# Attention outputs normalised in the attention stage on GpSimd, layer norm inside the turn plan, weight loads issued by ScalarE, output loads reordered

## The reference

```
s   = attention(xn)                    # 32 query heads, 8 key/value heads, head size 32, rotary, causal
g   = silu(ffn(xn))
out = x + s * g
```

```
t = layer_norm(xn)[:, -1, :] @ agg_w + agg_b
repeat 4 times: t = t + gelu(layer_norm(t) @ d1_w + d1_b) @ d2_w + d2_b
broadcast = t @ bc_w + bc_b
ffn = layer_norm(xn + sigmoid(xn @ gate_w + gate_b) * broadcast)
```

## Time and profile before

| | us |
|---|---|
| median of three runs | 2880.41 |
| profiled execution | 2904.24 |
| its span | 2902.5 |
| busy TensorE | 2643.2 (91%) |
| busy VectorE | 1714.5 (59%) |
| busy GpSimd | 1297.7 (45%) |
| busy ScalarE | 1055.4 (36%) |
| TensorE's mean granted clock | 0.954 |

### The profile page before, as it was taken

One profiled execution on the slowest core, in us unless ns is written; L12 is line 12 of the kernel. 1 busy time (PEld: TensorE's weight loads), 2 busy tenths in 40 slices (PEclk: granted clock), 3 DMA queues, 4 the chain that ended last, 5 costly groups with the idle time before them and its releaser, 6 DMA issues. The chain is left out here.

```text
span 2902.5 us, 46017 instructions
## 1 busy us (share of the span) xinstructions
PE 2643.2 (91%) x14400; PEld 1712.5 (59%) x14400; DVE 1714.5 (59%) x3448; ACT 1055.4 (36%) x1715; POOL 1297.7 (45%) x562
## 2 busy tenths in 40 slices
PE   5999999969999999999999999995688788898887
PEld 4888888844444444444444444442577676676775
DVE  6455444356555655566556655653666667676666
ACT  2111111106666565665666556662211111111111
POOL 0211211127788678877888688872111111111111
PEclk9999999979999999999999999997799999899998
DMA  6444444365654565556455545564678677567766
GB/s 232 167 175 172 166 173 174 138 201 182 189 154 152 166 189 153 153 167 186 152 156 167 184 152 157 167 189 137 138 123 116 111 123 123 111 124 124 123 114 121
DMA packets 235894, 450.04 MB, mean 155 GB/s; under 512 B 17528, under 2 KB 101720, under 8 KB 235860
## 3 DMA queue, kind: packets, MB, share of 16 engines
q1 hardware_dynamic: 162468, 397.68, 43.3%
q0 software_dynamic: 73392, 51.91, 14.4%
HBM read 334.42 MB, written 114.58 MB: 155 GB/s over the span
## 5 line engine op out<-in xcount | busy, mean ns | idle before, releaser
L867 DVE CUSTOM_DVE_ANT_0 bcast<-mxp,mask_q 128x128 f32<-128x128 f32 (+7 forms) x1054 | 751.9, 754 | 506.4 <-PE mxp L976 283.5
L796 ACT ACTIVATE pr<-stp 128x512 f32<-128x512 f32 x1152 | 670.3, 596 | 529.1 <-PE stp L985 351.6
L985 PE MATMUL stp<-qs,ks 97*128 97x512 f32 x1152 | 522.5, 461 | 19.2 <-ACT pr L796 14.8
L1385 PE MATMUL gp<-g,xa 128*128 128x512 f32 x1536 | 395.3, 421 | 128.9 <-DMA xa<-xt_scratch 117.5
L426 PE MATMUL eo<-xt,w 128*128 128x512 f32 x1920 | 449.2, 393 | 3.6 <-DVE xt L369 3.6
L749 POOL TENSOR_TENSOR acc<-acc,pr 128x2048 f32<-128x2048 f32 x96 | 439.7, 4580 | 24.7 <-ACT pr L796 14.5
L985 PEld LDWEIGHTS stp<-qs,ks 97*128 97x128 f32 x1152 | 214.7, 189 | 384.1 <-ACT pr L796 275.8
L1385 PEld LDWEIGHTS gp<-g,xa 128*128 128x128 f32 x1536 | 313.5, 206 | 210.1 <-issue 108.0
L426 PEld LDWEIGHTS eo<-xt,w 128*128 128x128 f32 x1920 | 359.1, 189 | 77.5 <-issue 4.0
L1385 PE MATMUL op<-o,ya 128*128 128x512 f32 x1536 | 356.2, 391 | 21.6 <-DVE ya L1326 21.6
L1385 PEld LDWEIGHTS op<-o,ya 128*128 128x128 f32 x1536 | 290.3, 189 | 82.6 <-DVE ya L1326 22.0
(11 more groups left out here) (139 smaller groups left out, 2788.0 us busy)
## 6 DMA issues: line engine op xcount, KB each, us to landing
wch<-in_d_w SPq DMA_DIRECT2D x132, 1024.0 KB, 8.0
qs<-q_scratch SPq DMA_DIRECT2D x201, 256.0 KB, 7.3
xa<-xt_scratch POOLq DMA_DIRECT2D x66, 512.0 KB, 9.0
xt_scratch<-xt SPq DMA_DIRECT2D x16, 2048.0 KB, 14.6
q_scratch<-r SPq DMA_DIRECT2D x64, 512.0 KB, 3.2
o_rinv<-r_scratch SPq DMA_DIRECT2D x33, 512.0 KB
yr<-y_scratch POOLq DMA_DIRECT2D x33, 512.0 KB, 6.5
xs<-in_x SPq DMA_DIRECT2D x33, 512.0 KB, 10.7
```

Of the source, the lines that this page charges most:

```text
L796: nc.scalar.activation(pr[half][:, :, at:at + P], stp[u % 2][:].rearrange("p (h t) -> p h t", h=REP), ACT.Exp, scale=SCALE).then_inc(act_d ...
L867: last = nc.vector.tensor_tensor_reduce(out=bcast[:, k % 2, hh * step:hh * step + w], in0=mxp[k % 2][:, hh * step:hh * step + w], in1=mask ...
L985: last = nc.tensor.matmul(bank, ks[par][:, j * P:(j + 1) * P], qs[par][:, :, i * P:(i + 1) * P], start=True, stop=i != j)
L1385: last = nc.tensor.matmul(bank[:, cols], lhs[pa][:, k, :], ws[pw][:, k, cols], start=(k == 0 and (pa, pw) == (0, 0)), stop=(k == KT - 1 an ...
```

## The change

The sums of a half are stored to a small `s_scratch` as soon as they are there, and loaded back as 128 partitions of 16 numbers (`spread_sums`); VectorE inverts these (`rc 1` in slot 27, `rc 0` in slot 33), SyncE stores the inverses and loads them repeated over each head's partitions (`spread_inverse`), and GpSimd multiplies `ys` with them (`normalise`) before y is stored: half 1 between its third and fourth large addition, half 0 after the fourth. SyncE's order of a turn changes with it: y of half 0 is now stored in the turn after, both spreads stand at the turn's end, ahead of the next turn's load of `ks`. The output stage drops its sums, inversion, spread load and multiplication.

The weights of the recurrent part are issued by ScalarE, behind its copy of the first burst and, for the second, behind the exponential of unit 12. In the last two turns of a step the layer norm is in the plan (`ls`, `l0`, `lc`, `l1`, `lv`, `lt`; only in the odd turn), for which the last iteration of the loop over chunks is unrolled (`turns`). In the output stage GpSimd waits for `y2_done` and issues `load_ya` ahead of `load_xa`.

```diff
@@ -81,21 +81,23 @@
 12: mx 5, pv 0 3, cy 0
 13: mx 6
 14: ss 1
-15: mx 7
+15: mx 7, ls
 16: mx 8
-18: mx 9
+18: mx 9, l0, lc
 19: mx 10, ge
 20: ss 0, mx 11
 21: pv 1 0, pv 1 1
 22: mx 12
 23: mx 13
-24: pv 1 2
+24: pv 1 2, l1, lv
 25: mt 0, mx 14
 26: mx 15
+27: rc 1
 28: pv 1 3, mx 16
 29: mx 17
 31: mx 18, pv 1 4
-33: mx 19
+32: lt
+33: mx 19, rc 0
 34: pv 1 5
...
+SPREAD = REP * HALF // P
...
+        sr = [sb(f"sr{i}", [P, SPREAD], F32) for i in range(2)]
+        rr = [sb(f"rr{i}", [P, SPREAD], F32) for i in range(2)]
+        rinv = [sb(f"rinv{i}", [P, HALF], F32) for i in range(2)]
...
-        use = {"fa": 0, ("mt", 1): 1, "fb": 2, "ft": 3, ("ss", 1): 4, ("ss", 0): 5, ("mt", 0): 6}
+        uses = [{"fa": 0, ("mt", 1): 1, "fb": 2, "ft": 3, ("ss", 1): 4, ("ss", 0): 5, ("mt", 0): 6},
+                {"fa": 0, ("mt", 1): 1, "fb": 2, "ft": 3, ("ss", 1): 4, "l0": 5, ("ss", 0): 6, "l1": 7, ("mt", 0): 8}]
+
+        def turns(engine, turn):
+            with engine.Fori(0, STEPS) as s:
+                with engine.Fori(0, CH - 1) as c:
+                    for par in range(2):
+                        turn(s, c, par, uses[0])
+                for par in range(2):
+                    turn(s, CH - 1, par, uses[par])
 
         def products(e, n):
...
-            def store_sums(half, slot):
-                sp.dma_start(s_d[:, bass.ds(slot, 1), half * HALF:(half + 1) * HALF].rearrange("h a t -> h (a t)"),
-                             sm[half][0:P:HD, :]).then_inc(s_out[half], 16)
+            def spread_sums(half, k, tu):
+                sp.wait_ge(tr_free, tu + 2)
+                sp.dma_start(s_d[half], sm[half][0:P:HD, :]).then_inc(s_out[half], 16)
+                sp.wait_ge(s_out[half], 16 * k + 17)
+                sp.dma_start(sr[half][:], s_d[half].rearrange("h (a u) -> (h a) u", u=SPREAD)).then_inc(sr_in[half], 16)
+
+            def spread_inverse(half, k):
+                sp.wait_ge(rc_done, 2 * k + 2 - half)
+                sp.dma_start(r_d[half].rearrange("h (a u) -> (h a) u", u=SPREAD), rr[half][:]).then_inc(r_out[half], 16)
+                sp.wait_ge(r_out[half], 16 * k + 17)
+                rows = r_d[half].unsqueeze(1)
+                sp.dma_start(rinv[half][:], rows.to_broadcast([REP, HD, HALF])).then_inc(rb_in[half], 16)
...
+                sp.wait_ge(st_done, NST * n + 2)
+                load_k(nxt, (n + 1) % GROUPS)
+                load_q(1, nxt, it if par == 0 else (it + 1) % (GROUPS // 2))
+                sp.wait_ge(pv_done, products((1, 7), n))
+                load_v(nxt, (n + 1) % GROUPS)
+                sp.wait_ge(tr_free, tb + use[("mt", 1)] + 2)
+                move_mt(1, par)
+                cn = (c + par) % CH
+                sp.wait_ge(yn_done, 2 * n + 1)
+                store_y(0, n)
+                sp.wait_ge(st_done, NST * n + HALF_ST + 1)
+                load_q(0, par, (it + 1) % (GROUPS // 2))
+                if par == 1:
+                    sp.wait_ge(hp_done, it + 1)
+                    sp.dma_start(b1c[:], d1_b[bass.ds(cn, 1)].rearrange("a p k -> (a p) k")).then_inc(b1_in, 16)
+                spread_sums(1, n, tb + use[("ss", 1)])
+                spread_sums(0, n, tb + use[("ss", 0)])
+                sp.wait_ge(tr_free, tb + use[("mt", 0)] + 2)
+                move_mt(0, nxt)
+                spread_inverse(1, n)
+                sp.wait_ge(yn_done, 2 * n + 2)
+                store_y(1, n)
+                spread_inverse(0, n)
+
+            turns(sp, turn)
             sp.wait_ge(tr_full, LAST)
             sp.dma_start(picks, pick).then_inc(c_in, 16)
...
+            spread_sums(1, GROUPS, LAST + 2)
+            spread_inverse(1, GROUPS)
+            sp.wait_ge(yn_done, 2 * GROUPS + 1)
+            store_y(0, GROUPS)
...
+            def normalise(half, n):
+                pool.wait_ge(ys_done, 2 * n + 3 - half)
+                pool.wait_ge(rb_in[half], 16 * (n + 1))
+                nc.gpsimd.tensor_tensor(ys[half][:], ys[half][:], rinv[half][:], ALU.mult).then_inc(yn_done, 1)
...
+                    nc.gpsimd.tensor_tensor(acc[:], other, pr[1][:, :, at:at + HALF], ALU.add).then_inc(add_done, 1)
+                    if j == 3:
+                        if "l1" in use:
+                            ln_pool(s + 1, tb + use["l1"])
+                        normalise(1, n)
...
+            def load_w(burst, c, cw, par):
+
+                for kh in range(2):
+                    r = kh * 512 + burst * 256
+                    src = d2_w[bass.ds(c * D + r, 256), :] if par == 0 else d1_w[r:r + 256, bass.ds(cw * D, D)]
+                    nc.scalar.dma_start(wch[burst][:, 2 * kh:2 * kh + 2, :],
+                                        src.rearrange("(k p) n -> p k n", p=P)).then_inc(w_in[burst], 16)
...
+                        if e[0] == "fc":
+                            copy_burst(tb + use["fa"])
+                            load_w(0, c, cw, par)
+                        elif e[0] == "ft":
+                            act.wait_ge(tr_full, tb + use["fb"] + 1)
+                            load_w(1, c, cw, par)
...
-            def layernorm_scale(tu, k, base):
-                dve.wait_ge(tr_full, tu + 2)
-                nc.vector.tensor_scalar(ve[:], trp[:, 0:B], EPS_F, None, ALU.add).then_inc(ln_ve, 1)
+            def layernorm_var(tu):
+                dve.wait_ge(tr_full, tu + 1)
+                nc.vector.tensor_scalar(ve[:], trp[:, 0:B], EPS_F, None, ALU.add).then_inc(tr_free, 1)
+
+            def layernorm_scale(k, base):
                 dve.wait_ge(ln_rs, k + 1)
-                nc.vector.tensor_tensor(cen[:], cen[:], rows(rs[:]), ALU.mult).then_inc(tr_free, 1)
-                dve.wait_ge(tr_free, tu + 3)
+                link(nc.vector.tensor_tensor(cen[:], cen[:], rows(rs[:]), ALU.mult), base)
                 link(nc.vector.tensor_tensor(cen[:], cen[:], bc(fvec[:, 1, :], B), ALU.mult), base)
                 nc.vector.tensor_tensor(t_in[:, :, 0:B], cen[:], bc(fvec[:, 2, :], B), ALU.add).then_inc(t_done, 1)
+
+            def reciprocals(half, k):
+                dve.wait_ge(sr_in[half], 16 * (k + 1))
+                dve.wait_ge(r_out[half], 16 * k + 1)
+                nc.vector.reciprocal(rr[half][:], sr[half][:]).then_inc(rc_done, 1)
 
...
+                        elif e[0] == "ls" and "l0" in use:
+                            link(nc.vector.tensor_tensor(th[:], th[:], bc(fvec[:, 3, :], B), ALU.add), base)
+                            layernorm_sum()
+                        elif e[0] == "lc" and "l0" in use:
+                            layernorm_centre(tb + use["l0"], base)
+                        elif e[0] == "lv" and "l1" in use:
+                            layernorm_var(tb + use["l1"])
+                        elif e[0] == "lt" and "l1" in use:
...
+                        elif e[0] in ("l0", "l1") and e[0] in use:
+                            k = int(e[0] == "l1")
+                            mean(tb + use[e[0]], s2 if k else s1, (s + 1) * 2 + k + 1)
...
-                for k, v in enumerate((s1, s2)):
-                    mean(TR0 + s * TR_STEP + NT * TRN + k, v, (s + 1) * 2 + k + 1)
...
             for n, (src, _, w2, k) in enumerate(pieces):
-                if n == 2:
-                    spread(0, 0)
-                    load_sums(1)
...
-                    spread(1 - par, n + 1)
-                    load_sums((n + 2) % TILES)
...
             with pool.Fori(0, TILES) as n:
+                pool.wait_ge(y2_done, n + 1)
+                load_ya((n + 1) % TILES)
                 pool.wait_ge(g_done, n + 1)
                 load_xa((n + 1) % TILES)
                 power(n, 0)
                 power(n, 1)
-                pool.wait_ge(y2_done, n + 1)
-                load_ya((n + 1) % TILES)
...
-            act.wait_ge(yn_done, 1)
+            act.wait_ge(ya_in, 16)
...
-                    act.wait_ge(yn_done, n + 2)
+                    act.wait_ge(ya_in, 16 * (n + 2))
...
-            normalise(0)
...
-                    invert(n + 1)
...
-                    normalise(n + 1)
```

More of the change, by code:

```diff
@@ L539, in attention_phase @@
         s_out = [sem(f"a_s_out{i}") for i in range(2)]
+        sr_in = [sem(f"a_sr_in{i}") for i in range(2)]
+        r_out = [sem(f"a_r_out{i}") for i in range(2)]
+        rb_in = [sem(f"a_rb_in{i}") for i in range(2)]
+        rc_done, yn_done = sem("a_rc"), sem("a_yn")
         b1_in, c_in = sem("a_b1_in"), sem("a_c_in")
@@ new lines, in turn @@
+            def turn(s, c, par, use):
+                it = s * CH + c
+                n = it * 2 + par
+                nxt = 1 - par
+                tb = trb(s, c, par)
+                sp.wait_ge(st_done, NST * n + 2)
[21 more added lines that the diff above has]
+                spread_inverse(0, n)
@@ L681, in _ @@
             for half in range(2):
-                sp.wait_ge(y_out[half], 16 * (GROUPS + half) + 1)
+                sp.wait_ge(y_out[half], 16 * (GROUPS + 1) + 1)
                 sp.wait_ge(s_out[half], 16 * (GROUPS + half) + 1)
@@ L751, in _ @@
```

(15 more changed lines are left out.)

379 lines of the change are left out of this document (149 added, 230 removed).

## The result

The changed kernel takes 2962.8 us (median of 4 runs, 2958.3 to 2969.6), the one before 2882.6 in the same measurement: ratio 1.029, 95% interval 1.026 to 1.031. It is slower; I had forecast 2842 and faster.

A forecast was written before the change was run, and what follows sets the result against it. TensorE was taken as the attention's bound, with some 55 of 400 us idle in the output stage. Terms -16 + 25 + 3 + 2 - 12 - 35 - 5 = -38 took 2880.4 to 2842 us; range 2770 to 2930, own range 2800 to 2872.

The forecast's parts named there:

- The chain of inverse sums on SyncE's queue: Attention turns: stores, waits and spread loads delay `ks`; TensorE waits 0.8 us per group, +25 us, bounds 0 and +93.
- rival A: Attention turns: spread loads land in 5 to 6 us, TensorE waits 3 us per group; 2912 us in all, chance 0.15.
- Weights' loads from ScalarE: Attention turns: issue time on ScalarE, 0 to 63 us if unhidden, nearly all hidden by its waits for TensorE: +3 us.
- Layer norm: Attention step ends: three gaps of 8.62 us between turns go, 3.3 us per step comes back: -16 us, between 0 and -23.
- Tiles: Output stage: spread load, reciprocal and multiplication go, `xa` still waits some 5 us every second tile: -35 us, bounds -105 and +16.
- Rival D: Output stage: all loads hide, 23.3 to 24.5 us per tile and no slow clock; 2762 us in all, chance 0.10.
- Rival B: Attention turns: VectorE's reciprocal waits for GpSimd's additions, 3.2 us per group; 2945 us in all, chance 0.15.
- Rival C: Output stage: loads in the new order collide as before, tiles +16 instead of -35; 2893 us in all, chance 0.10.
- Handover: Attention to output stage: spread hold, first multiplication and handshake go, `xa` of tile 1 comes later: -12 us, bounds -5 and -17.
- End of the attention: Stage end: bias product's input no longer waits behind a layer norm, but a last chain is added: +2 us, bounds -6 and +8.
- a wait for `acc`: Attention turns: two added GpSimd multiplications per group delay the late additions whose sum TensorE wants at slot 14: cost 0.
- End: Kernel's end: the last `yr` multiplication and its wait for a load, before the last store, go: -5 us.

The follow-up runs named there:

- the chain repaired: Changed kernel with both reciprocals in slot 27 and both stores, then both spread loads, behind the transposed maxima: 2809.0 us, ratio 0.974.
- the best kernel: Changed kernel with both inverses together in slot 27 and ScalarE's weight loads moved to slots 12 and 18: 2768.9 us, ratio 0.960.
- two stores: Kernel before, with SyncE held each turn by two 16 KB stores and their waits ahead of the `ks` load: 2966.5 us, ratio 1.030.
- four: Kernel before, with SyncE held each turn by four 16 KB stores and their waits ahead of the `ks` load: 3098.8 us, ratio 1.074.

## Why the prediction was wrong

**The step that failed: "The chain of inverse sums on SyncE's queue".** It had the right mechanism and place, and rival A said what comes of it. The term was +25 us, bounds 0 and +93; it measured 200 (2962.8 - 2763.3). Three durations in it were too short. From the first spread load to y's store, behind which the second chain stands, it took 6.3 to 6.7 us, where I had 5.0: the load took 4.8 to 5.2 to its use, and I took the 3.6 of a `ks` load for it. The second store and wait took 1.8 us, not 1.40, since y's store is ahead of it in the queue; I had taken, where nothing is ahead. So `ks` was issued 3.0 us later, not 1.3. And it landed in 4.4 to 6.3 us, not 3.6: I wrote that 256 KB now lie ahead of it and gave them no time. The wait is 5.0 us in the turn shown and 4.9 on average of the 28 turns that have one, not 0.8. A plain turn is 7.7 us longer (48.06 against 40.37), so 2.8 go beside the wait, with a clock of 0.93 for 0.99; a part of them may be the early weights', which this kernel doesn't separate. I priced a microsecond of wait at one, although the output stage showed what a wait does to the product behind it: held by stores alone, it cost 1.7 to 1.8. Rival A, with spread loads of 5 to 6 us, took 3 us per turn, for the same omissions. It named what happened; I gave it 0.15. (Its time is 2842 + 31 x 2.2 = 2910, not 2912, and B's 31 x 3.2 is 99, not 103; neither matters here.)

**Weights' loads from ScalarE: +3, measured +67 alone.** I asked whether ScalarE's time for the issue is hidden. It is, as far as TensorE's waits for ScalarE show; the cost is in where the first 2 of a turn's 4 MB now fall, before the move of the maxima and not behind it. SyncE's order had been holding them back, and I counted an issue but not its bytes. In the changed kernel this cost lies under the wait for `ks`, as late weights gained nothing there; with the chain repaired it comes out, 40 us.

**Layer norm: -16, measured between -5 and +3.** Step-end turns cost 6.9 us more than plain ones in the best kernel, 8.5 in the one before, 9.4 without the chain, three times each. In the changed kernel it is 1.1 us, but there a plain turn waits as long anyway. Two costs came back: the square, 3.2 us in the changed kernel, which I had at 3, and a stop of TensorE once behind each step's end, 2.6 us in the changed kernel and 2.9 without the chain, which I had not (below).

**Tiles: -35, measured -123 to -147.** Rival D, at 0.10, had it: its 23.3 to 24.5 us were still too many for 21.8. I took the spread load for a third of the collision and let the new order of `yr` cost 5 us of wait in every second tile. The landing of `xa` is 6.2 us after the change, and 5.2 with neither spread nor new order, inside the 11.0 us of the op product. The same size of load that I gave no time in the attention I gave too little here: a spread load costs the other transfers more than its share of bytes.

**The rest.** Handover -12, measured -19 between two profiles. End of the attention +2, measured +8.7, beyond its bound of +8: TensorE waits 11.5 us there for GpSimd's late additions, which stand behind two multiplications, each held 3.5 us or more by its spread load. I had put a wait for `acc` at nothing; inside the turns there is none. End -5, measured -5.5. Rival B is out: the reciprocal took 0.25 us in the midst of a GpSimd addition (1405.74 in 1403.30 to 1407.88). The Trainium skill ("SBUF — State Buffer", "Who interferes with whom") had said so, and its other half holds as well: the two-input square in the plan took 3.2 us beside GpSimd's addition, against 0.19 elsewhere. Rival C is out, as the tiles show.

The forecast's sign hung on two errors of opposite sign, 175 us in the chain and 88 to 112 in the tiles. With the size measured for the tiles and my own chain term I would have said 2730 to 2754, and been further off: that the miss was not larger is luck.

## What to carry to other kernels

A chain of store, wait and load on the queue that also issues the loads of the next turn is priced by what it delays, not by its own time: read off how long before its use each load behind it is issued, add the bytes put just ahead, and multiply the excess by what the reduced clock adds. Moving transfers to another engine's queue removes an order as well as issue time; where a small transfer is on the critical path, put the megabytes behind it by hand. Place a chain's transfers in the stretch in which the DMA engines are idle (here the second half of a turn): that made a loss of 2.9% into a gain of 2.6%, and of 4.0% with the weights late as well. And look at the DMA engines' share while a load runs by itself: the spread load's 0.26 leaves three quarters of the engines' time unused.

## What the runs showed of the hardware

A 256 KB load that spreads 4 rows over 128 partitions ran at 100 GB/s, with the 16 DMA engines busy for 0.26 of the time. Issued 0.95 us ahead of the pair of `ks` loads, it lengthened the landing of the second, of 128 KB, from 3.5 to 6.3 us. Without the 512 KB one per tile, `xa` landed in 5.2 us instead of 8.5 (both from 2300 to 2700), and a tile took 4.0 to 4.7 us less.

An 8 KB move took 5.2 us to its use while 2 MB ran on another engine's queue, and 9.5 with a spread load, `ks`, q and `vs` as well.

A wait of 1.54 us was enough for a granted clock of 0.50 behind it. A microsecond of wait cost 1.8 where a turn had 1.6 of it (two stores), and 1.7 where it had 4.4 (four).

TensorE stood still for 2.6 to 3.1 us, once after each step's end, in the changed kernel and its variants, where the trace shows nothing that it waited for. In the changed kernel without its chain:

```profile
983.44 0.49 PE L1040 MATMUL stp<-qs,ks 97*128 97x512 f32 x1 [2.89 <-issue]
```

The kernel before has three such stops of 0.4 to 0.5 us. It is the first turn of the inner loop again, after the turns that the change writes out in full; that the jump back over the longer code is the cause was not tried.
